# Expert tiles of 256 rows in place of 512, with the split of the weights shared by three engines

## The reference

```python
m = _layernorm(x, ln2_g, ln2_b)
xt = m.reshape(-1, Dd)                                   # 4096 x 256
probs = jax.nn.softmax(xt @ Wg, axis=-1)
wts, idx = jax.lax.top_k(probs, 2)
wts = wts / jnp.sum(wts, axis=-1, keepdims=True)
h1 = jax.nn.gelu(jnp.einsum('td,edf->etf', xt, W1) + b1[:, None, :])   # W1: 8 x 256 x 1024
ye = jnp.einsum('etf,efd->etd', h1, W2) + b2[:, None, :]               # W2: 8 x 1024 x 256
sel = ye[idx, jnp.arange(T)[:, None], :]
return x + jnp.sum(wts[..., None] * sel, axis=1)
```

## Time and profile before

| | us |
|---|---|
| median of 3 executions | 3681.22 (3680.1 to 3689.88) |
| the profiled execution | 3691.94 |
| its span, first to last instruction | 3690.2 |
| first up matmul of the expert loop | 3034.44 |
| end of the loop's last addition | 3583.96 |

### The profile page before, as it was taken

The page is one execution under the profiler, slowest core; times in us unless marked ns, Lnnn a source line. Parts: engine busy times, 40 slices in busy tenths (PEclk is TensorE's granted clock), DMA queues, the critical chain, the costliest instruction groups (busy, mean ns, idle before and its releaser), DMA issues. The chain is left out here.

```text
span 3690.2 us, 75025 instructions
## 1 busy us (share of the span) xinstructions
PE 3380.0 (92%) x27060; PEld 1746.7 (47%) x27060; DVE 2683.7 (73%) x5298; ACT 2707.4 (73%) x3030; POOL 1223.2 (33%) x1115
## 2 busy tenths in 40 slices
PE   7979999999999999999999999999997419999980
PEld 4534444444444444444444444444444419999970
DVE  1758999999999999999999999999973403333326
ACT  2328999999999999999999999999992105555540
POOL 0311212222222222212222222222213368888855
PEclk9959999999999999999999999999998559999995
DMA  3530101011010101101011010101002534444424
GB/s 107 206 70 20 30 22 31 20 32 29 21 32 21 30 22 31 30 22 31 20 32 30 21 32 20 31 21 31 20 17 101 179 113 137 142 139 135 136 81 127
DMA packets 165401, 218.76 MB, mean 59 GB/s; under 512 B 56960, under 2 KB 119808, under 8 KB 160640
## 3 DMA queue, kind: packets, MB, share of 16 engines
q1 hardware_dynamic: 146640, 186.07, 18.1%
q0 software_dynamic: 6336, 16.79, 1.4%
q10 hardware_dynamic: 12144, 12.06, 0.9%
HBM read 132.49 MB, written 68.94 MB: 55 GB/s over the span
## 5 line engine op out<-in xcount | busy, mean ns | idle before, releaser
L863 ACT ACTIVATE probs<-s_ps 128x1024 f32<-128x1024 f32 x2048 | 2012.4, 1023 | 186.2 <-PE s_ps L715 174.2
L904 DVE TENSOR_REDUCE unit_max<-m_ps 128x1 f32<-128x512 f32 x3072 | 1950.4, 685 | 242.5 <-PE m_ps L739 223.6
L765 PE MATMUL o_ps<-probs,v_here 128*32 128x256 f32 (+1 forms) x14336 | 1232.2, 422 | 0.3 <-ACT o_here L868 0.3
L715 PE MATMUL s_ps<-q_stage,k_ring 50*128 50x512 f32 x4096 | 930.8, 453 | 1.4 <-ACT probs L863 0.9
L739 PE MATMUL m_ps<-k_ring,q_stage 48*128 48x512 f32 x3584 | 928.0, 448 | 0.8 <-DVE unit_max L904 0.4
L739 PEld LDWEIGHTS m_ps<-k_ring,q_stage 48*128 48x128 f32 x3584 | 509.1, 187 | 440.7 <-DVE unit_max L904 329.2
L715 PEld LDWEIGHTS s_ps<-q_stage,k_ring 50*128 50x128 f32 x4096 | 402.0, 185 | 464.6 <-ACT probs L863 245.7
L765 PEld LDWEIGHTS o_ps<-probs,v_here 128*32 128x32 f32 x14336 | 296.6, 108 | 591.6 <-issue 392.8
L659 POOL TENSOR_TENSOR ctx_stage<-o_here,o_groups 17x512 f32<-17x512 f32 x128 | 162.5, 1270 | 988.6 <-DMA o_groups<-o_here 988.6
L1634 DVE TENSOR_TENSOR hidden_low<-h_ps,hidden_high 128x512 fp32r<-128x512 f32 x184 | 127.3, 692 | 366.4 <-ACT hidden_high L1598 366.4
L914 DVE CUSTOM_DVE_ANT_0 excess<-m_ps,excess 128x512 f32<-128x512 f32 x512 | 333.3, 689 | 29.8 <-issue 3.6
(11 more groups left out here) (179 smaller groups left out, 2749.8 us busy)
## 6 DMA issues: line engine op xcount, KB each, us to landing
w_in<-in_W SPq DMA_DIRECT2D x46, 1024.0 KB, 4.9
q_stage<-qs_dram SPq DMA_DIRECT2D x768, 32.0 KB, 1.8
o_groups<-o_here SPq DMA_DIRECT2D x384, 34.0 KB
k_ring<-ks_dram SPq DMA_DIRECT2D x96, 128.0 KB, 4.2
slots_dram<-zero_rows SPq DMA_DIRECT2D x24, 512.0 KB, 6.5
rows_e<-slots_dram SPq DMA_DIRECT2D x24, 512.0 KB, 3.9
y_slots_dram<-y_out ACTq DMA_DIRECT2D x23, 512.0 KB, 4.2
qs_dram<-parts SPq DMA_DIRECT2D x16, 512.0 KB, 2.8
```

Source lines behind the costliest of these rows:

```text
L715: last = nc.tensor.matmul(s_ps[:, at_ring % 2, k, :], k_ring[at:at + AROWS, par, P * t:P * t + P], q_stage[at:at + AROWS, buf * CHUNK:buf ...
L765: last = nc.tensor.matmul(o_ps[at:at + SQ, lo:hi], v_here[:, par, first_tile(t) + 2 * k, :], probs[:, t, k, lo:hi], start=(pair == 0), sto ...
L863: nc.scalar.activation(probs[:, t, :, :], s_ps[:, score_place(i, t) % 2, :, :], ACT.Exp).then_inc(s_read, 1)
L904: nc.vector.tensor_reduce(unit_max[:, n % 2, qt, 2 * j + k:2 * j + k + 1], m_ps[:, g % 3, :], AX.X, ALU.max).then_inc(m_read, 1)
```

## The change

Tiles have 256 rows (`ROWS_E`), so there are 39 of them. All buffers of rows, hidden units and results shrink to 256 rows; `up` has matmuls of 256 columns, `down` has 6 matmuls, and there are 4 transposes a tile. The loaded weights `w1_in` and `w2_in` have two buffers. GpSimd keeps the two roundings of W1. VectorE takes the two subtractions of W1 (behind f = 3 and 4) and the subtraction of W2 in two halves (behind f = 5 and 7); ScalarE takes the rounding of W2 in two halves (behind f = 2 and 3). The addition of `b2` moves from f = 3 to f = 2 in the loop's code (it stands ahead of that f's hidden subtraction). TensorE waits for W1 at the tile's start and for each half of W2 at down 0 and down 4. `dispatch` counts in tiles of 256, with slightly larger tables, and 20 zero fills of 512 rows take the place of 24.

```diff
-SLOT_TILES = (TOP * TOKENS + EXPERTS * (CHUNK - 1)) // CHUNK
+ROWS_E = 256
+TPE = ROWS_E // P
+SLOT_TILES = (TOP * TOKENS + EXPERTS * (ROWS_E - 1)) // ROWS_E
+MOST_TILES = TOKENS // ROWS_E
...
-            with sp.Fori(0, SLOT_TILES + 1) as j:
+            with sp.Fori(0, (SLOT_TILES + 1) * ROWS_E // CHUNK) as j:
...
             def load_bias(j, b):
-                sp.wait_ge(y_read, j * 2 + 2)
+                sp.wait_ge(y_read, j + 1)
...
                 sp.wait_ge(w1_split, j)
                 sp.sem_inc(sync_passed, 1)
-                sp.dma_start(w1_in[:, :, :], dram["W1"][ds(e, 1), :, :].rearrange("a (j p) f -> p (a j) f", p=P)
-                             ).then_inc(w1_full, 16)
+                sp.dma_start(w1_in[:, b, :, :], dram["W1"][ds(e, 1), :, :].rearrange("a (j p) f -> p (a j) f", p=P)
+                             ).then_inc(w1_full[b], 16)
...
                 pool.wait_ge(ups_done, j + 1)
-                pool.wait_ge(w1_full, j * 16)
-                w1 = w1_in[:, :, :].rearrange("p j (i t) -> p j t i", t=FT)
+                pool.wait_ge(w1_full[b], (j + b) * 8)
+                w1 = w1_in[:, b, :, :].rearrange("p j (i t) -> p j t i", t=FT)
                 for half in range(HALVES):
                     nc.gpsimd.tensor_tensor(w1_high[:, b, half, :, :], w1[:, half, :, :],
                                             zero[:, :].unsqueeze(2).to_broadcast([P, FT, P]), ALU.add
-                                            ).then_inc(w_ready, 1)
-                pool.wait_ge(w_ready, j * W_OPS + 2)
-                for half in range(HALVES):
-                    nc.gpsimd.tensor_tensor(w1_low[:, b, half, :, :], w1[:, half, :, :],
-                                            w1_high[:, b, half, :, :].bitcast(F32), ALU.subtract).then_inc(w_ready, 1)
...
-                nc.gpsimd.tensor_tensor(w2_high[:, b, :, :], w2_in[:, :, :],
-                                        zero[:, :].unsqueeze(2).to_broadcast([P, FT, D]), ALU.add).then_inc(w_ready, 1)
...
-                nc.gpsimd.tensor_tensor(w2_low[:, b, :, :], w2_in[:, :, :], w2_high[:, b, :, :].bitcast(F32),
-                                        ALU.subtract).then_inc(w_ready, 1)
...
+                                            ).then_inc(w1_rounded, 1)
...
-                pe.wait_ge(w_ready, j * W_OPS + 6)
+                pe.wait_ge(w1_ready, j * 2 + 2)
...
+            def high_w2(j, b, part):
+
+                if part == 0:
+                    act.wait_ge(hidden_used, j * FT + (4 - FT))
+                    act.wait_ge(w2_full[b], (j + b) * 8)
+                    act.sem_inc(act_passed, 1)
+                some = slice(FT // 2 * part, FT // 2 * part + FT // 2)
+                nc.scalar.activation(w2_high[:, b, some, :], w2_in[:, b, some, :], ACT.Copy).then_inc(w2_rounded, 1)
...
+                    if f in (2, 3):
+                        high_w2(j + 1, 1 - b, f - 2)
...
+            def low_w1(j, b, half):
+
+                dve.wait_ge(w1_rounded, j * 2 + (half - 1))
+                w1 = w1_in[:, b, half, :].rearrange("p (i t) -> p t i", t=FT)
+                nc.vector.tensor_tensor(w1_low[:, b, half, :, :], w1, w1_high[:, b, half, :, :].bitcast(F32),
+                                        ALU.subtract).then_inc(w1_ready, 1)
...
+            def low_w2(j, b, part):
+
+                dve.wait_ge(w2_rounded, j * 2 + (part - 1))
+                some = slice(FT // 2 * part, FT // 2 * part + FT // 2)
+                nc.vector.tensor_tensor(w2_low[:, b, some, :], w2_in[:, b, some, :], w2_high[:, b, some, :].bitcast(F32),
+                                        ALU.subtract).then_inc(w2_ready, 1)
...
             def tile(j, b, first):
                 for f in range(FT):
-                    if f == 3 and not first:
+                    if f == 2 and not first:
                         add_b2(j - 1, 1 - b)
                     dve.wait_ge(high_done, j * FT + (f + 1))
                     nc.vector.tensor_tensor(hidden_low[:, f % 4, :], h_ps[:, f % 2, :],
                                             hidden_high[:, f % 4, :].bitcast(F32), ALU.subtract).then_inc(low_done, 1)
+                    if f == 3:
+                        low_w1(j + 1, 1 - b, 0)
+                    if f == 4:
+                        low_w1(j + 1, 1 - b, 1)
+                    if f == 5:
+                        low_w2(j + 1, 1 - b, 0)
                     if f == 6:
                         low_rows(j + 1, 1 - b)
+                    if f == 7:
+                        low_w2(j + 1, 1 - b, 1)
...
-            keep["w1_in"] = left(whole, "w1_in", [P, HALVES, FF])
-            keep["w2_in"] = left(whole, "w2_in", [P, FT, D])
+            keep["w1_in"] = left(whole, "w1_in", [P, 2, HALVES, FF])
+            keep["w2_in"] = left(whole, "w2_in", [P, 2, FT, D])
```

More of the change, by code:

```diff
@@ L1256, in dispatch @@
         rank = sb("rank", [P, TILES, EXPERTS])
-        starts = sb("starts", [P, EXPERTS])
+        starts = sb("starts", [P, MOST_TILES])
         table = sb("table", [P, EXPERTS, EXPERTS])
+        reached = sb("reached", [P, EXPERTS, MOST_TILES])
         tiles_of = sb("tiles_of", [P, EXPERTS])
@@ L1336, in _ @@
             do(nc.vector.tensor_tensor(rank[:, :, :], rank[:, :, :], within_ps, ALU.add))
[L1338 to L1342, removed]
+            do(nc.vector.tensor_scalar(starts[:, :], count[:, 0:MOST_TILES], float(ROWS_E), None, ALU.mult))
+            square, oblong = [P, EXPERTS, EXPERTS], [P, EXPERTS, MOST_TILES]
+            do(nc.vector.tensor_tensor(reached[:, :, :], sums[:, now, TILES - 1, :].unsqueeze(2).to_broadcast(oblong),
+                                       starts[:, :].unsqueeze(1).to_broadcast(oblong), ALU.is_gt))
+            do(nc.vector.tensor_reduce(tiles_of[:, :], reached[:, :, :], AX.X, ALU.add))
             do(nc.vector.tensor_tensor(table[:, :, :], experts_row.to_broadcast(square),
@@ L1388, in experts @@
         bias2 = sb("bias2_e", [P, HALVES])
[L1389 to L1392, removed]
+        rows = sb("rows_e", [P, 2, TPE, D])
+        mT = sb("mT_e", [P, HALVES, ROWS_E])
+        m_high = sb("m_high", [P, 2, HALVES, ROWS_E], F32R)
+        m_low = sb("m_low", [P, 2, HALVES, ROWS_E], F32R)
         w1_in, w2_in = keep["w1_in"], keep["w2_in"]
@@ L1521, in turn @@
                 for half in range(HALVES):
-                    for t in range(TPC):
+                    for t in range(TPE):
                         last = nc.tensor.transpose(tr_ps[:, half, P * t:P * t + P], rows[:, b, t, P * half:P * half + P],
@@ L1537, in down @@
                 if f == 0:
-                    pe.wait_ge(y_read, j * 2 + 2)
-                for t in range(TPC):
+                    pe.wait_ge(y_read, j + 1)
+                if f % (FT // 2) == 0:
+                    pe.wait_ge(w2_ready, j * 2 + (2 * f // FT + 1))
+                for t in range(TPE):
                     cols = slice(P * t, P * t + P)
                     for n, (h, w) in enumerate(((hidden_high, w2_high), (hidden_high, w2_low), (hidden_low, w2_high))):
-                        last = nc.tensor.matmul(y_ps[:, b, t // 2, D * (t % 2):D * (t % 2) + D], h[:, f % 4, cols],
-                                                w[:, b, f, :], start=(f == 0 and n == 0 and t % 2 == 0),
+                        last = nc.tensor.matmul(y_ps[:, b, D * t:D * t + D], h[:, f % 4, cols],
+                                                w[:, b, f, :], start=(f == 0 and n == 0 and t == 0),
                                                 stop=(f == FT - 1 and n == 2), skip_group_check=True)
@@ L1572, in _ @@
             act.sem_inc(low_done, 2)
-            act.sem_inc(y_read, 4)
+            act.sem_inc(y_read, 2)
             act.wait_ge(affine_in, 2 * 16)
```

81 lines of the change are left out of this document (40 added, 41 removed).

## The result

| | before | after |
|---|---|---|
| median, us | 3681.44 (3680.1 to 3689.88, 4 executions) | 3841.39 (3826.5 to 3842.54, 4 executions) |
| ratio after to before | | 1.042, 95% interval 1.039 to 1.045 |
| the profiled execution (span) | 3691.94 (3690.2) | 3841.29 (3839.4) |
| first up matmul to end of the last addition | 549.5 | 702.8 |
| pitch of a tile | 23.74, 23 tiles | 17.97, 39 tiles |

The kernel is slower by 160 us, 4.2%. The forecast was 3795, which is 114 us slower; the range of 3700 to 3850 holds the time.

What follows compares the result with a forecast made beforehand. TensorE's stream was taken to bound the old kernel. Afterwards 39 tiles x 17.07 = 666 us, less 549.5, less 2.5, gives +114 on the median: 3795 us; own range 3775 to 3815, wide range 3700 to 3850 (0.85).

Steps and rivals of the forecast that it cites:

- the rival of the lost clock: TensorE's clock halves after the 2.8 us gap: about 1.1 us more a tile, 18.2 us, 3839 us; chance 0.13.
- Step 1: Tile's start: GpSimd's second rounding blocks VectorE's second W2 subtraction 2.25, which then runs, then hidden subtraction 0: 3.90 us.
- Step 2: Next in the tile: TensorE's up 2, ScalarE's Gelus, copies and W2 rounding, to hidden subtraction 3: 4.33 us.
- Step 3: On VectorE alone: two W1 subtractions at 1.91 and hidden subtractions 4 and 5, TensorE waiting: 4.59 us.
- 4, to the end of the row subtraction: Tile's end: up 7, then GpSimd's rounding starts first and blocks the row subtraction for 2.25: 4.25 us.
- The block: In the expert loop, GpSimd's roundings and VectorE instructions with two SBUF operands exclude each other, 2.25 us each time.
- The race: At the tile's end GpSimd's rounding starts 0.09 us before the row subtraction could, so the latter waits.
- The rival's 14.9: Row subtraction starts before GpSimd at the tile's end, only the second W2 subtraction blocked: pitch 14.9 us, 3711; chance 0.25.
- 14.0 without a block: GpSimd and VectorE don't block each other in the loop, TensorE's order binds: pitch 14.0 us, 3675; chance 0.08.
- 13.3 with W1 contiguous: No blocking in the loop and W1 subtractions at the contiguous 1.215 us: pitch 13.3, 3648 us; chance 0.04.
- TensorE's 12.1: TensorE stays the expert loop's bound at 12.1 us a tile: 3601 us; chance 0.03.
- The break-even at 14.15: Pitch of the expert tiles from which the changed kernel gets faster than before: 14.15 us.

Runs made afterwards that it cites:

- experiment 4: The changed kernel with 20 extra matmuls of 256 columns in TensorE's gap before each tile's first up, into an unread PSUM bank: 3828.72 us, ratio 1.0398 to before.
- experiment 1: The changed kernel with one more wait: GpSimd's two W1 roundings start only after the row subtraction is done: 3759.26 us, ratio 1.0197 to before.
- experiment 2: The changed kernel with GpSimd's two W1 roundings held back until the second W2 subtraction is done: 3696.49 us, ratio 1.0036 to before.
- the second probe: The changed kernel with the first tile's W1 subtractions repeated in `dispatch` beside TensorE's loop-type matmuls, those plus ScalarE copies, and ScalarE alone: 3857.51 us.
- version 3: The changed kernel with GpSimd's roundings behind the second W2 subtraction and W1 read in stored order, two PSUM buffers for h: 3651.16 us, ratio 0.9910 to before.
- version 2: The changed kernel with experiment 2's wait, W1 in stored order, more h, hidden and `y_out` buffers, downs four behind, VectorE's pieces reordered: 3609.1 us, ratio 0.9796 to before.
- experiment 3: The changed kernel with VectorE reading W1 contiguously in `low_w1` (wrong elements), nothing else altered: 3768.66 us, ratio 1.0224 to before.

## Why the prediction was right and where it was wrong

The mechanism came as forecast, and its size was too small. The forecast's own range, 3775 to 3815, does not hold the 3841. The wide range does, because it was drawn up to 3850 for the rival of the lost clock; that this rival's price was 3839 is luck, since experiment 4 shows that the clock is not what the forecast lacked.

The four steps of its walk can be laid on the tile of the timeline above. Row subtractions end at 3302.20 and 3320.22; hidden subtractions 0, 3 and 5 end at 3306.66, 3310.75 and 3315.96. That tile has 4.46, 4.09, 5.21 and 4.26, 18.02 in all. With the tile ahead of it and the two behind it (those of the four windows), read in the same way:

| step | forecast | mean of four tiles |
|---|---|---|
| 1, blocked W2 subtraction to hidden subtraction 0 | 3.90 | 4.28 |
| 2, to hidden subtraction 3 | 4.33 | 4.23 |
| 3, the two W1 subtractions to hidden subtraction 5 | 4.59 | 5.19 |
| 4, to the end of the row subtraction | 4.25 | 4.24 |
| pitch | 17.07 | 17.94 |

- *The block* was right, and it carries the result: experiments 1 and 2 take away its two halves, 2.00 and 1.58 us a tile. The Trainium skill's stricter rule (SBUF — State Buffer, "SBUF: two separate sides": the first comer keeps the pair for its whole instruction) agrees at least as well as the taken 2.25. The row subtraction came free 2.3 us after GpSimd's start, of an instruction of 2.42; in experiment 1 the second W2 subtraction stood for up to 2.40 (3.62 less 1.22).
- *The race* went as forecast, with 0.12 us in place of 0.09. The rival's 14.9 for the other outcome was 15.97 in experiment 1; the difference lies in steps 1 to 3 there too.
- *Step 1* lacked a wait. VectorE waits for its own second W2 result before it tells SP that the buffer is free: 0.24 us, and 0.54 where a round of the loop ends, that is in every second tile (the hidden subtraction's copy was long done, at 3304.36, when it started at 3306.24). The walk had such a wait in step 3, but priced it there at no more than a lost overlap, and had none here.
- *Step 2* was 0.24 too long in the tiles at full clock, since two of ScalarE's instructions overlap the one ahead by 0.1 each, as VectorE's do; a fall of the clock gives part of it back.
- *Step 3* is the term that was mis-sized. The W1 subtractions take 2.19, not 1.99, and the wait for the own result 0.22 more. The 1.99 came from a row where TensorE stood idle; in the second probe the same subtraction takes 2.18 beside TensorE at the loop's rate and ScalarE, and 2.01 beside ScalarE alone.
- *The clock* was a rival at 1.1 us a tile. It did fall, in two of the four tiles shown, and cost 0.14 a tile, because the blocked W2 subtraction covers most of the slow matmuls (the clock is at half from 3321.5 to 3324.5, and that subtraction runs from 3320.47 to 3323.67). The Trainium skill warns of idle gaps between bursts (TensorE: Matmul & The Clock Gate, "Why this matters for your kernels"); the trace agrees in these two tiles, behind gaps of 2.81 and 2.75 us, and not in the other two, behind gaps of 2.79 and 2.74. The gaps that the page means are longer than these, so by it alone the chance need not have been higher, as the prediction has it. In the earlier trace rows the clock stayed full for over four us of a pause.
- *The sum.* 0.87 us a tile too little is 34 of the 37 us by which the loop is longer than the forecast 666; the rest is mostly at its two ends. To the medians some 10 us more come from the choice of the profiled execution: that of before lies 10.5 us over its median, that of after on it. The first up came 2.2 us earlier, for which 2.5 was forecast.
- *The other rivals' prices* were good where experiments built them: 14.0 without a block was 14.39 (the W1 term for the most part), 13.3 with W1 contiguous was 13.22 in version 3, TensorE's 12.1 was 12.18 in version 2, with 3609 us where 3601 was given. The break-even at 14.15 holds too: at 14.39 the kernel is slower by 0.36%.

## What to carry to other kernels

When work moves from a free engine into gaps of engines that stand in a short chain, compare each piece with one step of that chain and not with the engine's idle time: with steps of 2.83 us the shared split left a tile at TensorE's own 23.74 us, and with steps of 1.43 it made the tile 17.97 us where TensorE's own work is 12.18 (version 2). Of these 5.8 us the meetings at the port are 3.6. If GpSimd and VectorE both read two SBUF operands, order them by a wait, since here one added wait on GpSimd was worth 145 us. Take the price of a strided read from a row in which TensorE runs.

## What the runs showed of the hardware that was not expected

- A VectorE subtraction of 1,024 elements with one operand at a stride of 32 bytes takes 1.99 us with TensorE idle and 2.18 beside TensorE at full rate and ScalarE. Contiguous it takes 1.22 with TensorE idle (the first tile of version 2) and 1.215 in the loop (experiment 3). The Trainium skill (SBUF — State Buffer, the paragraph on cachelines in "Door 1: The DMA port swizzle") says that each access that crosses to a new line of 16 bytes pays a penalty, which agrees with the first price. The same page ("SBUF: two separate sides") has the port pair of VectorE and GpSimd as the only place of contention among the engines; for a strided read the second probe speaks against that, since TensorE and ScalarE have no part in the pair and the read became longer beside them.
- GpSimd's rounding of 1,024 elements is 1.89 us contiguous (versions 2 and 3). With the stride it is 2.42 at its shortest and 2.66 in the median of experiment 2, where no VectorE instruction with two SBUF operands meets it; what makes these 0.24 us was not asked.
